# Five elementwise multiplies of a Mamba and MLP layer moved from the Vector engine to GpSimd

## The chip, the cores and the metric

The kernel runs on the 8 cores of one Trainium2 chip. Each core does the same program on its own half of one sequence, with no exchange between cores. The metric is the device time of the slowest core in microseconds (us). TensorE is called PE below, VectorE DVE, ScalarE ACT, GpSimd POOL and SyncE SP.

## The reference

One "sandwich" layer on x of shape (4, 2048, 2048), float32. LN is a layer norm without weights.

```python
# attention half: LN, then a Mamba-like block with its own layer norm, then residual
a  = LN(x)
p  = layer_norm(a, ln_w, ln_b) @ in_proj_W.T              # 2048 -> 96
u  = silu(conv1d(p, conv_w, width 3) + conv_b)
d, Bp, Cp = split(u @ x_proj_W.T, [6, 16, 16])
delta = softplus(d @ dt_proj_W.T + dt_proj_b) * 0.001
s_t = exp(delta*A) * s_(t-1) + delta*Bp*u                 # 96 x 16 states, scanned over 2048 steps
y   = sum_n(s_t * Cp) + u*D
x  = x + LN(y @ out_proj_W.T + a)
# MLP half
z  = LN(x)
w  = sum(softmax(top2(z @ router.T)))                     # one weight per token
f  = mlp(z; 8192 hidden) + mlp(z; 1024 hidden) * w        # mlp: silu(z@g.T) * (z@u.T) @ d.T
x  = x + LN(f)
```

## The kernel before

All code sits in one function, `build_program`, written against a small scheduler class `Sched`. `S.op(engine, emit, reads, writes, waits)` appends one instruction to the stream of the engine named by its first argument, and turns the reads and writes of the named resources into semaphore waits. The waits don't depend on the engine: also two instructions of one engine that depend on each other wait through a semaphore. Every engine runs its stream in the order of the program text. `S.fence()` makes every engine wait for all that came before it. Features lie on the partitions and tokens on the free axis; each core owns 1024 tokens, handled as tiles of 128x512.

The stages in order of time:

- Mixer, 0 to 443 us. The core computes the scan over 2048 tokens plus a halo, in five chunks `c` of 512. For each chunk: statistics and the input projection, then, one chunk behind (`pc = c - 1`), the convolution, the gate and the projections to `dus_bf` and `du_bf`. `du_bf` is masked by a multiply with `m96k` at L685 (`ts_`). Then a loop over 12 groups `j` of 8 channels by 16 states: PE expands delta (L707) and `du` (L714) to 128 rows; ACT makes the exponential `dA` (L711); DVE makes `dBu` from PSUM (L718), runs the scan (L722) and saves the last state (L726). For the two chunks with `pc >= 2`, whose outputs the core keeps, DVE multiplies the states by C (L730, `tj7`, written in place of `dA`) and PE sums over the states with a float32 matmul (L733). In PE's stream L733 of group j stands ahead of L707 and L714 of group j+1.
- O stage, 444 to 755 us, in two passes `hc` of 512 tokens. First part, loop `mc` of 16: output projection on PE (L815, L817); DVE scales the residual from the loaded `x_half` by a broadcast row (L823, `t_s`, into one of two buffers) and adds it to PSUM (L826); ACT casts and squares; PE sums the statistics (L762, L767). Second part, loop `k` of 16: DVE multiplies `mr_sb` by the broadcast reciprocal deviation (L841, `tx1`), POOL adds the broadcast mean term (L845, `tx2`), DVE adds the residual (L849, `tx3`). All three name one resource `r_mr` for the whole of `mr_sb`, so `tx1` of tile k+1 waits for `tx3` of tile k. The result is stored to HBM.
- Normalization stage, 755 to 836 us, in two passes of 16 tiles: an ACT-queue DMA loads a tile into one of two buffers `x2t` (L911), DVE multiplies (L914, `tz1`) and adds into the bf16 `z4_sb` (L917, `tz2`). The load into a buffer waits for `tz2` of the tile that used it last.
- Router and small MLP (836 to 1100 us), the gate and up projections of the large MLP (1100 to 1998 us), its down projection (to 2570 us), and an end stage that normalizes and writes out (to 2766 us).

POOL's stream also issues DMAs: the chunk loads (L522, called from L595) in the mixer, and the weight loads (L1003, L1005 and later).

Of the kernel before, what the change touches and what calls it, by code (L numbers as in the profile page):

```python
# [24 lines left out]
ENG_SEM = {"tensor": "s_pe", "scalar": "s_act", "vector": "s_dve",  # L25
           "gpsimd": "s_pool", "sync": "s_sy"}
# [14 lines left out]
class Sched:  # L41
    def __init__(self):
        self.ops = []
        self.cnt = {}
        self.pending = {}
        self.dma_idx = {q: 0 for q in DMA_SEMS}

    def _mk(self, eng, emit, waits, inc_sem, inc_by):
        if eng in self.pending:
            waits = list(waits) + self.pending.pop(eng)  # L50
        self.cnt[inc_sem] = self.cnt.get(inc_sem, 0) + inc_by
        tok = (inc_sem, self.cnt[inc_sem], eng)
        best = {}
        for wt in waits:
            if wt is None:
                continue
            s, v, peng = wt
            if best.get(s, -1) < v:
                best[s] = v
        wl = sorted(best.items())  # L60

        def run(e, emit=emit, wl=wl, inc=(inc_sem, inc_by)):
            for s, v in wl:
                e.wait_ge(_SEMS[s], v)
            inst = emit(e)
            inst.then_inc(_SEMS[inc[0]], inc[1])
        self.ops.append((eng, run))
        return tok

# [130 lines left out]
def build_program(debug_taps=()):  # L200
    global _SEMS
    nc = bass.Bass("TRN2", target_bir_lowering=False)
# [76 lines left out]
    du_bf = at("s_dub", (96, 512), BF16, WB0 + 4096)  # L279
    m96k = [at(f"s_m96k{i}", (96, 512), F32, WB0 + 5120 + 2048 * i) for i in range(2)]  # L280
# [107 lines left out]
    S = Sched()  # L388
# [72 lines left out]
    def tap(name, ap_src, waits, reads=(), q="sync"):  # L461
        if name in taps:
            out_toks.append(S.dma(q,
                                  lambda e, a=ap_src, d=taps[name]: e.dma_start(out=d, in_=a),
                                  reads=reads, waits=waits))

    const_toks = []
    for dst, src in [(ident, ident_h), (ones1x128, ones1x128_h),
                     (ones1x128bf, ones1x128bf_h), (ones128bf, ones128bf_h),
# [36 lines left out]
    def mm_wpsum(e):  # L506
        for k in range(KC):
# [4 lines left out]
    t_wpsum = S.op("scalar", lambda e: e.activation(wpsum_bf[:], pb[6][0:1, 0:96], AF.Copy),  # L512
                   reads=[r_pb[6]], waits=[tk])

    x3 = xT.rearrange("(k p) t -> p k t", p=128)
    t_xbf = [None] * NCHUNK

# [12 lines left out]

    for c in range(NCHUNK):
        cc = c % 2
        def mm_sx(e, cc=cc):
            for k in range(KC):
                i = e.matmul(pb[0][0:1, :], ones128bf[:], xcb[cc][:, 512 * k:512 * (k + 1)],
                             start=(k == 0), stop=(k == KC - 1))
            return i
        t_sx = S.op("tensor", mm_sx, reads=[r_xcb[cc]], writes=[r_pb[0]],
                    waits=[t_xbf[c]] + CW)
        for k in range(KC):  # L540
            kk = k % 2
# [75 lines left out]
        if c == 2:  # L617
# [8 lines left out]
        tap(f"xp{c}", xp_all[0:96, 1 + 512 * c:1 + 512 * (c + 1)], [t3_],  # L626
            reads=[r_xp[c]])

        pc = c - 1
        if pc < 0:  # L630
            continue
        pcc = pc % 2
# [49 lines left out]
        tr_ = S.op("vector", lambda e, pcc=pcc: e.scalar_tensor_tensor(  # L682
                       du_bf[:], dus_bf[:], 0.001, u_ch[pcc][:, :], ALU.mult, ALU.mult),
                   reads=[r_dus, r_u[pcc]], writes=[r_dub], waits=[tq])
        ts_ = S.op("vector", lambda e, pcc=pcc: e.tensor_mul(du_bf[:], du_bf[:], m96k[pcc][:]),  # L685
                   reads=[r_m96[pcc]], writes=[r_dub], waits=[tr_])

        tt = S.op("tensor", lambda e: e.matmul(pb[6][:, :], selBbf[:], dbc_bf[:],
# [11 lines left out]
                       reads=[r_pb[6]], writes=[r_C[pcc]], waits=[tv])  # L700

        y_last = None
        for j in range(NJ):
            jb = j % 2
            bs = 3 if jb == 0 else 6
            bs2 = 4 if jb == 0 else 7
            tj1 = S.op("tensor", lambda e, j=j, bs=bs: e.matmul(  # L707
                           pb[bs][:, :], selDbf[:, 128 * j:128 * (j + 1)], dus_bf[:],
                           start=True, stop=True),
                       reads=[r_dus], writes=[r_pb[bs]], waits=[tq])  # L710
            tj2 = S.op("scalar", lambda e, j=j, jb=jb, bs=bs: e.activation(  # L711
                           dA_b[jb][:], pb[bs][:, :], AF.Exp, scale=A2[:, j:j + 1]),
                       reads=[r_pb[bs]], writes=[r_dA[jb]], waits=[tj1, t_A2])
            tj3 = S.op("tensor", lambda e, j=j, bs2=bs2: e.matmul(  # L714
                           pb[bs2][:, :], selDbf[:, 128 * j:128 * (j + 1)], du_bf[:],
                           start=True, stop=True),
                       reads=[r_dub], writes=[r_pb[bs2]], waits=[ts_])
            tj4 = S.op("vector", lambda e, jb=jb, pcc=pcc, bs2=bs2: e.tensor_mul(  # L718
                           dBu_b[jb][:], pb[bs2][:, :], Bp_bc[pcc][:]),
                       reads=[r_pb[bs2], r_Bp[pcc]], writes=[r_dBu[jb]], waits=[tj3, tu_])  # L720
            init = 0.0 if pc == 0 else state_cols[:, j:j + 1]
            tj5 = S.op("vector", lambda e, jb=jb, init=init: e.tensor_tensor_scan(  # L722
                           xs_b[jb][:], dA_b[jb][:], dBu_b[jb][:], init, ALU.mult, ALU.add),
                       reads=[r_dA[jb], r_dBu[jb]] + ([r_state[j]] if pc > 0 else []),
                       writes=[r_xs[jb]], waits=[tj2, tj4])
            tj6 = S.op("vector", lambda e, j=j, jb=jb: e.tensor_copy(  # L726
                           state_cols[:, j:j + 1], xs_b[jb][:, 511:512]),
                       reads=[r_xs[jb]], writes=[r_state[j]], waits=[tj5])
            if pc >= 2:
                tj7 = S.op("vector", lambda e, jb=jb, pcc=pcc: e.tensor_mul(  # L730
                               prod_b[jb][:], xs_b[jb][:], C_bc[pcc][:]),
                           reads=[r_xs[jb], r_C[pcc]], writes=[r_dA[jb]], waits=[tw_, tj6])
                tj8 = S.op("tensor", lambda e, j=j, jb=jb: e.matmul(  # L733
                               pb[2][0:96, :], selR_sb[:, 96 * j:96 * (j + 1)], prod_b[jb][:],
                               start=(j == 0), stop=(j == NJ - 1)),
                           reads=[r_dA[jb]], writes=[r_pb[2]] if j == 0 else [],
                           waits=[tj7] + CW)
                if j > 0:
                    r_pb[2].w = tj8
                y_last = tj8  # L740
# [9 lines left out]
                 reads=[r_yf], writes=[r_ybf], waits=[ty1])  # L750
    tap("yf", y_f[0:96, :], [r_ybf.w], reads=[r_yf])

    S.fence()

    def stats_tile(src_f32, first, last, wtok, par=0):
# [49 lines left out]
    for hc in range(2):  # L805
# [5 lines left out]
        for mc in range(KC):  # L811
            bank = 2 if mc % 2 == 0 else 5

            def mm_op1(e, mc=mc, off=off, bank=bank):
                e.matmul(pb[bank][:, :], outTbf[:, 128 * mc:128 * (mc + 1)],  # L815
                         y_bf[:, off:off + 512], start=True, stop=False)
                return e.matmul(pb[bank][:, :], ones1x128bf[:], nm1r1bf[:, off:off + 512],  # L817
                                start=False, stop=True)
            t_op = S.op("tensor", mm_op1, reads=[r_ybf, r_nm1r1], writes=[r_pb[bank]],
                        waits=CW)  # L820
            bcb_i = bc_b if mc % 2 == 0 else bc_b2
            r_bcb_i = r_bcb if mc % 2 == 0 else r_bcb2
            t_s = S.op("vector", lambda e, mc=mc, bcb_i=bcb_i: e.tensor_mul(  # L823
                           bcb_i[:, :], x_half[:, 512 * mc:512 * (mc + 1)], bc_a[:, :]),
                       reads=[r_xhalf, r_bca], writes=[r_bcb_i], waits=[t_xh, t_r1b])
            t_mr = S.op("vector", lambda e, mc=mc, bank=bank, bcb_i=bcb_i: e.tensor_add(  # L826
                            mr_sb[:, 512 * mc:512 * (mc + 1)], pb[bank][:, :], bcb_i[:, :]),
                        reads=[r_pb[bank], r_bcb_i], writes=[r_mr] if mc == 0 else [],
                        waits=[t_op, t_s])
            if mc > 0:  # L830
                r_mr.w = t_mr
            stats_tile(mr_sb[:, 512 * mc:512 * (mc + 1)], mc == 0, mc == KC - 1, [t_mr],
                       par=mc % 2)
# [4 lines left out]
        t_nm3b = bcast(bc_b, r_bcb, row(R_T2), r_rows[R_T2], [t_nm3], 4)  # L838
        for k in range(KC):
            kk = k % 2  # L840
            tx1 = S.op("vector", lambda e, k=k: e.tensor_mul(  # L841
                           mr_sb[:, 512 * k:512 * (k + 1)], mr_sb[:, 512 * k:512 * (k + 1)],
                           bc_a[:, :]),
                       reads=[r_bca], writes=[r_mr], waits=[t_r3b])
# [57 lines left out]
    for hc in range(2):  # L902
# [6 lines left out]
        for k in range(KC):  # L909
# [1 line left out]
            trl = S.dma("scalar", lambda e, k=k, kk=kk, off=off: e.dma_start(  # L911
                            out=x2t[kk][:], in_=x2_st[k, :, off:off + 512]),
                        writes=[r_x2t[kk]], waits=[r_x2st[k]])
            tz1 = S.op("vector", lambda e, kk=kk: e.tensor_mul(  # L914
                           x2t[kk][:], x2t[kk][:], bc_a[:, :]),
                       reads=[r_bca], writes=[r_x2t[kk]], waits=[trl, t_r4b])
            tz2 = S.op("vector", lambda e, k=k, kk=kk, off=off: e.tensor_add(  # L917
# [6 lines left out]
    tap("x2st", x2_st[:, :, :].rearrange("a b c -> (a b) c"), list(r_x2st))  # L924
    tap("z4t", z4_sb[:, :], [r_z4.w], reads=[r_z4], q="gpsimd")

    snapO = S.snapshot()
    S.fence_from(snapO)
    t_lge = [None, None]
# [64 lines left out]
    tap("combt", comb_bc[:, :], [r_combbc.w], reads=[r_combbc])  # L994
    tap("lgtt", lgt_tm[:, :], [r_lgttm.w], reads=[r_lgttm])

    S.fence_from(snapO)
    t_wrg = [None] * NRI
    t_wru = [None] * NRI
# [77 lines left out]

    tap("frst", fr_st[:, :, :].rearrange("a b c -> (a b) c"), list(r_frst))

    S.fence()  # L1080
    t_stash_done = r_x2st[KC - 1]
    t_wg = [None] * NI
# [11 lines left out]
    for i in range(NI):  # L1094
# [33 lines left out]
        if i + 2 < NI:  # L1128
            sched_wdma(i + 2)

    S.fence()
    t_wd = [[None, None] for _ in range(KC)]
    t_fr = [None] * KC
# [16 lines left out]
    for dt in range(KC):  # L1150
# [68 lines left out]
        if dt + 2 < KC:  # L1219
            sched_fdma(dt + 2)  # L1220

    S.fence()
    ep_r5 = [eprow(0), eprow(1)]
    ep_nm5 = [eprow(2), eprow(3)]
# [97 lines left out]
                    fn(e)  # L1322

    es.close()
    return nc


# [24 lines left out]
```

## Time and profile before

| | |
|---|---|
| median of the two runs | 2918.3 us (2768.13 and 3068.48) |
| the profiled execution, its own time | 2767.94 us |
| its span, first to last instruction of the slowest core | 2766.4 us |
| spans of the 8 cores | 2748.4 to 2766.4 us |
| busy: PE / ACT / DVE / POOL | 1923.9 / 466.3 / 396.3 / 355.4 us |

Busy time is a sum over the span; it doesn't say which engine is waited for in a stage. The chain of waits does: it is followed back from the last instruction, at each step to what released it. In a timeline row the first number is the start, the second the duration, both in us from the start of the span; the bracket at the end gives how long the engine stood idle ahead of the instruction and what released it. The two runs of before lie 11% apart; the profiled execution is of the lower kind, and all cores of it show about the same granted clock (0.802 to 0.806).

### The profile page before, as it was taken

What the parts mean: (1) busy time and instruction counts of PE and PEld (TensorE: products, weight loads), DVE (VectorE), ACT (ScalarE), POOL (GpSimd) and SP (SyncE); (2) the same over time, 40 slices, a digit from 0 to 9 for tenths busy, and PEclk for the clock granted to TensorE, in tenths of its full rate; (3) what the DMA queues carried; (4) which work ended last, traced back from release to release, by engine and by line L of the source; (5) the groups of instructions that cost most, each with busy time, mean ns of one, the idle gap of its engine ahead of it and who ended that gap; (6) DMA issues with size and microseconds to landing.
All of it is one profiled execution on the core that took longest, in us unless ns stands there. A gap on an engine that the chain in (4) does not pass through costs nothing.

```text
span 2766.4 us, 27032 instructions; the slowest of 8 cores (2748.4 to 2766.4 us)
## 1 busy us (share of the span) xinstructions
PE 1923.9 (70%) x7719; PEld 780.5 (28%) x7719; DVE 396.3 (14%) x589; ACT 466.3 (17%) x802; POOL 355.4 (13%) x400
## 2 busy tenths in 40 slices
PE   4444533434404976999999999999888888888200
PEld 2111100000002432444444444444333333333100
DVE  0553342232352100000000000000000000000222
ACT  3333211232301111111111111111100000000100
POOL 1000000020200210222222222222200000000122
PEclk9555555555556998999999999999989999999655
DMA  7220001030131435444444444444344444343233
GB/s 113 42 31 0 0 0 61 8 115 1 64 111 38 77 77 129 83 76 77 77 77 76 77 77 77 77 77 76 69 84 91 92 92 91 86 93 73 99 137 136
DMA packets 67530, 203.23 MB, mean 73 GB/s; under 512 B 7420, under 2 KB 17789, under 8 KB 63302
## 3 DMA queue, kind: packets, MB, share of 16 engines
q0 software_dynamic: 38608, 124.49, 26.0%
q10 hardware_dynamic: 18432, 50.34, 5.1%
q1 hardware_dynamic: 10358, 26.68, 2.7%
q8 instruction: 78, 1.28, 0.2%
q14 instruction: 54, 0.44, 0.1%
HBM read 292.41 MB, written 33.55 MB: 118 GB/s over the span
## 4 chain that ended last, share of the span: by engine, by line
PE 65%; DVE 11%; DMA 9%; issue 6%; ACT 4%; POOL 3%; DVEq 0%; SPq 0%; ACTq 0%; POOLq 0%
PE pb L1103 16%; PE pb L1112 16%; PE pb L1156 5%; PE pb L1159 4%; PE pb L1171 4%; PE pb L1174 4%; DMA s_epf<-f_stash 3%; PE pb L1019 2%; PE pb L1028 2%; DVE s_xs L722 2%; PE pb L733 2%; DMA s_x2t<-x_stash 2%; PE pb L1061 2%; DMA s_rdbuf<-Wrd 2%; POOL s_mr L845 1%
## 5 line engine op out<-in xcount | busy, mean ns | idle before, releaser
L1103 PE MATMUL pb<-s_z,s_gbuf 128*128 128x512 bf16 x2048 | 464.4, 380 | 13.4 <-DMA s_ubuf<-Wu 13.4
L1112 PE MATMUL pb<-s_z,s_ubuf 128*128 128x512 bf16 x2048 | 462.9, 379 | 0.0
L1103 PEld LDWEIGHTS pb<-s_z,s_gbuf 128*128 128x128 bf16 x2048 | 200.7, 98 | 256.3 <-issue 15.8
L1112 PEld LDWEIGHTS pb<-s_z,s_ubuf 128*128 128x128 bf16 x2048 | 200.4, 98 | 241.7
L1188 DVE TENSOR_TENSOR s_fstg<-pb,s_frbuf 128x512 f32<-128x512 f32 x32 | 20.6, 686 | 1551.6 <-PE pb L1174 1551.6
L1124 POOL TENSOR_TENSOR s_h<-s_gs,s_us 128x512 bf16<-128x512 bf16 x128 | 147.1, 1149 | 678.6 <-ACT s_us L1121 678.6
L1156 PE MATMUL pb<-s_h,s_dbuf 128*128 128x512 bf16 x512 | 210.7, 411 | 17.2 <-issue 16.9
L1159 PE MATMUL pb<-s_h,s_dbuf 128*128 128x512 bf16 x512 | 209.6, 409 | 0.0
L1171 PE MATMUL pb<-s_h,s_dbuf 128*128 128x512 bf16 x512 | 194.0, 379 | 4.1 <-PE pb L1159 4.1
L1174 PE MATMUL pb<-s_h,s_dbuf 128*128 128x512 bf16 x512 | 194.0, 379 | 0.0
L1118 ACT ACTIVATE s_gs<-pb 128x512 bf16<-128x512 f32 x128 | 76.4, 597 | 378.4 <-PE pb L1103 360.5
L1121 ACT ACTIVATE s_us<-pb 128x512 bf16<-128x512 f32 x128 | 76.4, 597 | 367.8 <-PE pb L1112 367.8
L845 POOL TENSOR_TENSOR s_mr<-s_mr,s_bcb 128x512 f32<-128x512 f32 x32 | 40.4, 1262 | 550.1 <-ACT s_bcb L797 495.3
L1196 ACT ACTIVATE s_fbf<-s_fstg 128x512 bf16<-128x512 f32 x32 | 20.1, 629 | 532.2 <-DVE s_fstg L1188 530.5
L733 PE MATMUL pb<-s_dA,s_selR 128*96 128x512 f32 x48 | 47.8, 1100 | 81.9 <-DVE s_dA L730 81.9
L1061 PE MATMUL pb<-s_rh,s_rdbuf 128*128 128x512 bf16 x256 | 69.2, 438 | 31.4 <-DMA s_rdbuf<-Wrd 31.4
L1136 POOL DMA_DIRECT2D s_dbuf<-Wd x32 | 17.0, 531 | 521.0 <-PE pb L1159 314.9
L1156 PEld LDWEIGHTS pb<-s_h,s_dbuf 128*128 128x128 bf16 x512 | 53.5, 105 | 93.1 <-issue 42.7
L762 PE MATMUL pb<-s_castb,s_o128b 128*1 128x512 bf16 x32 | 18.7, 585 | 78.0 <-ACT s_castb L758 78.0
L1159 PEld LDWEIGHTS pb<-s_h,s_dbuf 128*128 128x128 bf16 x512 | 53.2, 104 | 68.2 <-issue 17.3
L1171 PEld LDWEIGHTS pb<-s_h,s_dbuf 128*128 128x128 bf16 x512 | 50.0, 98 | 70.1 <-issue 11.5
L1174 PEld LDWEIGHTS pb<-s_h,s_dbuf 128*128 128x128 bf16 x512 | 50.1, 98 | 58.5
(192 smaller groups left out, 1468.9 us busy)
## 6 DMA issues: line engine op xcount, KB each, us to landing
s_gbuf<-Wg POOLq DMA_DIRECT2D x64, 512.0 KB, 5.9
s_ubuf<-Wu POOLq DMA_DIRECT2D x64, 512.0 KB, 7.8
s_dbuf<-Wd POOLq DMA_DIRECT2D x32, 1024.0 KB, 8.5
s_xcb<-xT POOLq DMA_DIRECT2D x5, 2048.0 KB, 15.6
s_xhalf<-xT SPq DMA_DIRECT2D x2, 4096.0 KB, 14.0
x_stash<-s_x2t ACTq DMA_DIRECT2D x32, 256.0 KB, 2.0
s_x2t<-x_stash ACTq DMA_DIRECT2D x32, 256.0 KB, 2.8
fr_stash<-s_frstg ACTq DMA_DIRECT2D x16, 512.0 KB, 5.5
```

The lines of the kernel that those rows point to most:

```text
L733: tj8 = S.op("tensor", lambda e, j=j, jb=jb: e.matmul(pb[2][0:96, :], selR_sb[:, 96 * j:96 * (j + 1)], prod_b[jb][:], start=(j == 0), stop ...
L845: tx2 = S.op("gpsimd", lambda e, k=k: e.tensor_add(mr_sb[:, 512 * k:512 * (k + 1)], mr_sb[:, 512 * k:512 * (k + 1)], bc_b[:, :]), reads=[r ...
L1061: i = e.matmul(pb[bank][:, :], rdbuf[db][:, 128 * ikr:128 * (ikr + 1)], r_h_sb[:, 1024 * ikr + hof:1024 * ikr + hof + 512], start=(ikr == ...
L1103: i2 = e.matmul(pb[bg][:, :], gbuf[ib][:, 128 * k:128 * (k + 1)], z4_sb[:, 1024 * k + hof:1024 * k + hof + 512], start=(k == 0), stop=(k = ...
L1112: i2 = e.matmul(pb[bu][:, :], ubuf[ib][:, 128 * k:128 * (k + 1)], z4_sb[:, 1024 * k + hof:1024 * k + hof + 512], start=(k == 0), stop=(k = ...
L1118: tsl = S.op("scalar", lambda e, half=half, bg=bg: e.activation(gs_t[half][:], pb[bg][:, :], AF.Silu), reads=[r_pb[bg]], writes=[r_gs[half ...
L1121: tuc = S.op("scalar", lambda e, half=half, bu=bu: e.activation(us_t[half][:], pb[bu][:, :], AF.Copy), reads=[r_pb[bu]], writes=[r_us[half ...
L1124: S.op("gpsimd", lambda e, i=i, hof=hof, half=half: e.tensor_mul(h_all[:, 1024 * i + hof:1024 * i + hof + 512], gs_t[half][:], us_t[half][:]),
L1156: e.matmul(pb[b0][:, :], dbuf[0][:, 128 * ik:128 * (ik + 1)], h_all[:, 1024 * ik:1024 * ik + 512], start=(ik == 0), stop=False)
L1159: i2 = e.matmul(pb[b1][:, :], dbuf[0][:, 128 * ik:128 * (ik + 1)], h_all[:, 1024 * ik + 512:1024 * (ik + 1)], start=(ik == 0), stop=False)
L1171: e.matmul(pb[b0][:, :], dbuf[1][:, 128 * (ik - 32):128 * (ik - 31)], h_all[:, 1024 * ik:1024 * ik + 512], start=False, stop=(ik == NI - 1))
L1174: i2 = e.matmul(pb[b1][:, :], dbuf[1][:, 128 * (ik - 32):128 * (ik - 31)], h_all[:, 1024 * ik + 512:1024 * (ik + 1)], start=False, stop=(i ...
```

## The change

Five `S.op` calls change their engine from `"vector"` to `"gpsimd"`, with operands, resources and waits unchanged: L685 (4 instructions), L730 (24), L823 (32), L841 (32) and L914 (32), in all 124. The rest of the diff records a phase name and an instruction count while the program is built; it emits no instruction.

```diff
-        def run(e, emit=emit, wl=wl, inc=(inc_sem, inc_by)):
+        ph = self.phase
+
+        def run(e, emit=emit, wl=wl, inc=(inc_sem, inc_by), ph=ph, eng=eng):
+            n0 = e.bass.n_instructions() if hasattr(e, "bass") else None
             for s, v in wl:
                 e.wait_ge(_SEMS[s], v)
             inst = emit(e)
             inst.then_inc(_SEMS[inc[0]], inc[1])
+            n1 = e.bass.n_instructions() if n0 is not None else None
+            self.dbg_map[eng].append((n1 - n0 if n0 is not None else 1 + len(wl), ph))
...
-        ts_ = S.op("vector", lambda e, pcc=pcc: e.tensor_mul(du_bf[:], du_bf[:], m96k[pcc][:]),
+        ts_ = S.op("gpsimd", lambda e, pcc=pcc: e.tensor_mul(du_bf[:], du_bf[:], m96k[pcc][:]),
...
-                tj7 = S.op("vector", lambda e, jb=jb, pcc=pcc: e.tensor_mul(
+                tj7 = S.op("gpsimd", lambda e, jb=jb, pcc=pcc: e.tensor_mul(
                                prod_b[jb][:], xs_b[jb][:], C_bc[pcc][:]),
...
-            t_s = S.op("vector", lambda e, mc=mc, bcb_i=bcb_i: e.tensor_mul(
+            t_s = S.op("gpsimd", lambda e, mc=mc, bcb_i=bcb_i: e.tensor_mul(
                            bcb_i[:, :], x_half[:, 512 * mc:512 * (mc + 1)], bc_a[:, :]),
...
-            tx1 = S.op("vector", lambda e, k=k: e.tensor_mul(
+            tx1 = S.op("gpsimd", lambda e, k=k: e.tensor_mul(
                            mr_sb[:, 512 * k:512 * (k + 1)], mr_sb[:, 512 * k:512 * (k + 1)],
                            bc_a[:, :]),
...
-            tz1 = S.op("vector", lambda e, kk=kk: e.tensor_mul(
+            tz1 = S.op("gpsimd", lambda e, kk=kk: e.tensor_mul(
                            x2t[kk][:], x2t[kk][:], bc_a[:, :]),
```

## Rows read from the trace of the kernel before

**Rows 1.** The page: span, and the chain that ended last, by engine.
```profile
span 2766.4 us, 27032 instructions; the slowest of 8 cores (2748.4 to 2766.4 us)
...
PE 65%; DVE 11%; DMA 9%; issue 6%; ACT 4%; POOL 3%; DVEq 0%; SPq 0%; ACTq 0%; POOLq 0%
```

**Rows 2.** Windows: stretch, its length, busy time of each engine, clock, DMA.
```profile
240.00:318.00 78.00, 34.28 (x50) 8.22 (x49) 34.02 (x49) 12.38 (x19) 0.00 (x0) 0.50 0.00 0
...
544.00:596.00 52.00, 19.15 (x32) 2.41 (x31) 22.15 (x32) 18.77 (x33) 20.19 (x16) 0.50 0.20 77
...
749.00:796.00 47.00, 8.33 (x10) 2.49 (x10) 23.21 (x34) 4.12 (x7) 0.00 (x0) 0.50 0.29 93
796.00:836.00 40.00, 0.00 (x0) 0.00 (x0) 22.24 (x34) 1.19 (x2) 0.00 (x0) 0.50 0.37 105
...
1100.00:1998.00 898.00, 885.68 (x4096) 401.06 (x4096) 0.00 (x0) 152.85 (x256) 215.49 (x257) 0.99 0.42 76
```

**Rows 3.** Groups of instructions by form, DVE: count, busy us, mean ns, idle before.
```profile
L841 DVE TENSOR_TENSOR s_mr<-s_mr,s_bca 128x512 f32<-128x512 f32 x32 | 22.2, 693 | 9.8 <-DVE s_x2t L849 5.2 <-ACT s_bca L797 4.6
...
L914 DVE TENSOR_TENSOR s_x2t<-s_x2t,s_bca 128x512 f32<-128x512 f32 x32 | 22.1, 690 | 34.8 <-DMA s_x2t<-x_stash 34.5
...
L730 DVE TENSOR_TENSOR s_dA<-s_xs,s_C 128x512 f32<-128x512 f32 x24 | 16.6, 693 | 2.5
```

**Rows 4.** Groups of instructions by form, POOL, same columns.
```profile
L845 POOL TENSOR_TENSOR s_mr<-s_mr,s_bcb 128x512 f32<-128x512 f32 x32 | 40.4, 1262 | 550.1 <-ACT s_bcb L797 495.3 <-DVE s_mr L841 54.9
...
L1040 POOL TENSOR_TENSOR s_rhtmp<-s_gs,s_us 128x512 bf16<-128x512 bf16 x16 | 18.4, 1147 | 133.9 <-ACT s_us L1037 133.9
```

**Rows 5.** Chain of waits, group loop with `pc >= 2`: start, us, what.
```profile
262.71 0.17 DVE s_state L726
...
262.97 0.70 DVE s_dA L730
...
263.81 1.99 PE pb L733 x2
...
269.20 0.70 DVE s_dA L730
```

**Rows 6.** Timeline around the masking multiply L685.
```profile
246.32 0.69 DVE L685 TENSOR_TENSOR s_dub<-s_dub,s_m96k 96x512 bf16<-96x512 bf16 x1
...
247.26 0.58 PE L714 MATMUL pb<-s_dub,s_selDb 96*128 96x512 bf16 x1 [0.98 <-DVE s_dub L685]
```

**Rows 7.** Timeline, O stage, first part, one period.
```profile
465.32 0.68 DVE L823 TENSOR_TENSOR s_bcb<-s_xhalf,s_bca 128x512 f32<-128x512 f32 x1
...
469.69 0.69 DVE L826 TENSOR_TENSOR s_mr<-pb,s_bcb 128x512 f32<-128x512 f32 x1 [3.69 <-PE pb L817]
```

**Rows 8.** Chain of waits, O stage, second part, one period.
```profile
547.93 0.70 DVE s_x2t L849
...
548.80 0.70 DVE s_mr L841
...
549.64 1.27 POOL s_mr L845
...
551.00 0.70 DVE s_x2t L849
```

**Rows 9.** Timeline, normalization stage, first pass.
```profile
764.22 0.69 DVE L914 TENSOR_TENSOR s_x2t<-s_x2t,s_bca 128x512 f32<-128x512 f32 x1
...
765.01 0.69 DVE L917 TENSOR_TENSOR s_z<-s_x2t,s_bcb 128x512 bf16<-128x512 f32 x1
767.01 0.69 DVE L914 TENSOR_TENSOR s_x2t<-s_x2t,s_bca 128x512 f32<-128x512 f32 x1 [1.31 <-DMA s_x2t<-x_stash]
767.81 0.69 DVE L917 TENSOR_TENSOR s_z<-s_x2t,s_bcb 128x512 bf16<-128x512 f32 x1
768.76 0.69 DVE L914 TENSOR_TENSOR s_x2t<-s_x2t,s_bca 128x512 f32<-128x512 f32 x1 [0.26 <-DMA s_x2t<-x_stash]
...
771.37 0.69 DVE L914 TENSOR_TENSOR s_x2t<-s_x2t,s_bca 128x512 f32<-128x512 f32 x1 [1.12 <-DMA s_x2t<-x_stash]
```

**Rows 10.** Timeline, end stage, where POOL and DVE share a tile.
```profile
2602.47 2.34 POOL L1271 TENSOR_TENSOR s_epf<-s_epf,s_frbuf 128x1024 f32<-128x1024 f32 x1 [9.30 <-DVE s_epf L1268]
2604.91 1.23 DVE L1274 TENSOR_TENSOR s_epo<-s_epf,s_epx 128x1024 f32<-128x1024 f32 x1 [2.58 <-POOL s_epf L1271]
```

More of the change, by code:

```diff
@@ L46, in __init__ @@
         self.dma_idx = {q: 0 for q in DMA_SEMS}
+        self.phase = "init"
+        self.dbg_map = {e: [] for e in ENG_SEM}
     def _mk(self, eng, emit, waits, inc_sem, inc_by):
@@ L465, in tap @@
                                   reads=reads, waits=waits))
+    S.phase = "prolog"
     const_toks = []
@@ L513, in build_program @@
                    reads=[r_pb[6]], waits=[tk])
+    S.phase = "mixer"
     x3 = xT.rearrange("(k p) t -> p k t", p=128)
@@ L532, in build_program @@
         cc = c % 2
+        S.phase = "mstat"
         def mm_sx(e, cc=cc):
@@ L627, in build_program @@
             reads=[r_xp[c]])
+        S.phase = "postxp"
         pc = c - 1
@@ L702, in build_program @@
         y_last = None
+        S.phase = "jloop"
         for j in range(NJ):
@@ L751, in build_program @@
     tap("yf", y_f[0:96, :], [r_ybf.w], reads=[r_yf])
+    S.phase = "O"
     S.fence()
@@ L925, in build_program @@
     tap("z4t", z4_sb[:, :], [r_z4.w], reads=[r_z4], q="gpsimd")
+    S.phase = "router"
     snapO = S.snapshot()
@@ L995, in build_program @@
     tap("lgtt", lgt_tm[:, :], [r_lgttm.w], reads=[r_lgttm])
+    S.phase = "routed"
     S.fence_from(snapO)
@@ L1078, in build_program @@
     tap("frst", fr_st[:, :, :].rearrange("a b c -> (a b) c"), list(r_frst))
+    S.phase = "gu"
     S.fence()
@@ L1129, in build_program @@
             sched_wdma(i + 2)
+    S.phase = "down"
     S.fence()
@@ L1220, in build_program @@
             sched_fdma(dt + 2)
+    S.phase = "ep"
     S.fence()
@@ L1324, in build_program @@
     es.close()
+    nc._dbg_sched = S
     return nc
```

## The prediction

> **What bounds the kernel now.** I read the page's chain of waits first. PE carries 65% of it, DVE 11% and POOL 3% [rows 1], so most of the span can't be touched by a change of DVE and POOL. The windows by stage show where it can. From 1100 to 1998 us PE is busy 885.68 of 898 us at a granted clock of 0.99, and DVE has not one instruction there [rows 2]. All five edits lie ahead of 836 us, where the rows show a granted clock of 0.50, the 1.2 GHz level, and where no engine is full: in 240 to 318 us PE is busy 34 and DVE 34 of 78 us; in 544 to 596 us DVE 22 and POOL 20 of 52 us; in 749 to 836 us DVE 45 of 87 us [rows 2]. Stages in which nobody is full are bound by a chain that goes round the engines. So the question for each moved multiply is whether it is a link of that chain, not how busy DVE is. The chain of waits and the timelines of each stage answer it. The fences behind this part pass any delay on whole.
>
> **The price of one multiply.** On DVE a 128x512 float32 multiply takes 0.69 us (693, 693 and 690 ns) [rows 3]. POOL has no float32 multiply in the trace. The nearest rows are its float32 add of the same shape, 1.262 us, and its bf16 multiply, 1.147 us [rows 4]. I take the add, since element size and ports match: +0.57 us for each; with the bf16 row +0.46. Handing over costs little: DVE to POOL 0.14 us (548.80 + 0.70 to 549.64), POOL to DVE 0.09 us (549.64 + 1.27 to 551.00), DVE to DVE through a semaphore 0.17 us (547.93 + 0.70 to 548.80) [rows 8], and 0.09 us from L726 to L730 [rows 5]. POOL to POOL and POOL to PE don't occur; I take the same 0.1 to 0.15, with 0 and 0.25 as bounds.
>
> **L730, 24 instructions: on the path.** The round of the group loop is 269.20 - 262.97 = 6.23 us. L733 starts 0.14 us after L730 ends, and L707 and L714 of the next group stand behind L733 in PE's stream, so DVE's next L718 can't start early either, however free DVE is [rows 5]. Nothing covers the longer multiply: 0.57 for it and 0.05 for the hand-over from L726 (0.14 in place of 0.09), 0.62 x 24 = 14.9 us.
>
> **L685, 4 instructions: on the path.** L685 ends at 247.01 and L714 starts at 247.26, released by it [rows 6]; L714 starts the group loop. At 0.69 now and 1.15 to 1.26 on POOL that is about 0.55 each, 2.2 us. POOL's only other work there is the issue of chunk loads. Each of those waits for L591 of its own chunk, which stands in PE's stream ahead of the group loop that a multiply feeds; none is queued between a ready multiply and PE.
>
> **L823, 32 instructions: hidden, but for two.** In the steady round of 5.0 us (465.32 to 469.69, and the 0.6 us from an L826 to its L823) DVE does L823 and then stands idle 3.69 us until PE's L817 releases L826 [rows 7]. The two buffers let POOL do L823 right after the L826 before, so 1.26 us lies under some 4.3 us of other work. Only the first of each pass is exposed, since it waits for the load of `x_half`: 2 x 0.6 = 1.2 us. Without the cover all 32 would be seen, 18 us. The time that DVE gains is worth nothing, as DVE waits for PE there.
>
> **L841, 32 instructions: on the path.** The round is L849 0.70, gap 0.17, L841 0.70, gap 0.14, L845 1.27, gap 0.09: 3.07 us from 547.93 to 551.00 [rows 8]. It looks as if POOL could now do tile k+1 while DVE does tile k. It can't: L841 writes `r_mr`, which L849 of the tile before has read, so it waits for it. After the change the round is L849, hand-over, L841 on POOL, hand-over, L845, hand-over: the same three gaps, one link 0.57 longer. The first L841 of a pass is covered by the broadcast that L845 waits for. 2 x 15 rounds x 0.57 = 17.1 us. With the hand-over bounds it is 14 to 22.
>
> **L914, 32 instructions: on the path once for two tiles.** With two buffers a buffer's round is load, L914, L917, and the next load only then. From the end of L917 at 768.50 to the next L914 at 771.37 are 2.87 us for the load; the round of a pair is 771.37 - 767.01 = 4.36 us [rows 9]. After the change it is 2.87 + 1.26 + 0.10 + 0.69 = 4.92 and a little for the wait, +0.6. The other buffer's work fits between, as POOL has 2.5 us of work for a pair. Each pass has 7 rounds and an end that is 0.53 longer: 2 x (7 x 0.6 + 0.53) = 9.5 us. The weight loads behind L914 in POOL's stream wait for the last L917 anyway.
>
> **The sum.** 14.9 + 2.2 + 1.2 + 17.1 + 9.5 = 44.9 us on the profiled execution's own 2767.9 us (span 2766.4): 2812.8 us, or 1.6% longer. The median of the two runs shown, 2918.3 us, is a mean of 2768.13 and 3068.48; my numbers stand against the first, with which the profiled execution agrees.
>
> **Rival 1, slower by over 2%: POOL and DVE shut each other out in the normalization stage.** There alone the change lets a POOL instruction and a DVE instruction that reads two SBUF tensors want to run at once: L914 of the second tile of a pair on POOL and L917 of the first on DVE. In the end stage the two only alternate [rows 10], the O stage's second part is serial [rows 8], and so no row shows what an overlap costs. If whichever starts first holds the other off, POOL wins, because its next L914 needs no hand-over: L917 of the first tile then starts 1.26 us later. The pair's tiles would be loaded about 0.6 us apart; the second load needs 3.06 us against 2.87 (765.70 to 768.76) [rows 9], so it lands about 0.8 us behind the first, inside the 1.26 us of the first L914, and the clash comes back every round. That is the point which decides: a second load landing more than 1.26 us late would end it. Round: 4.36 + 0.57 + 1.26 = 6.2 us; 2 x (7 x 1.84 + 1.1) = 28 us in place of 9.5, total 63.4, 2831.3 us. For it speaks that the pair's data are nearly simultaneous; against it, that no row shows a mutual stop. The Trainium skill, "SBUF — State Buffer", section "Who interferes with whom", says that a DVE instruction with two SBUF inputs contends with a GpSimd instruction that reads SBUF, the one that starts first keeping the other out for its whole length; by it this rival would hold. No run here shows it yet.
>
> **Rival 2: multiplies at the bf16 row's price.** At 1.147 us each of the some 75 exposed multiplies saves 0.11, about 8 us: 2804 us.
>
> **Rival 3, no cost: the second part of the O stage overlaps.** If tile k+1 on POOL didn't wait for tile k on DVE, the round would be POOL's 2 x 1.26 = 2.52 us in place of 3.07, -16.5 where I have +17.1: 2779 us. The resource `r_mr` speaks against it. A gain elsewhere would need a stage that DVE bounds, and there is none [rows 2].
>
> **How the numbers follow.** Forecast 0.48, rival 1 0.40, rival 2 0.06, rival 3 0.03, and 0.03 for a larger loss (hand-overs at their upper bound, or POOL's multiply slower than its add). The predicted time is the forecast's, 2813 us. The range takes in rival 2 with the lower hand-overs (2800) and rival 1 with hand-overs 0.1 us longer at some 75 places (2839): 2800 to 2840. The forecast's own range is 2801 to 2822. Two per cent, about what a measurement of this kernel can tell from no change, lie at 2823 us. Slower by over 2%: nearly all of rival 1 and the larger loss, 0.42. Within 2%: 0.57. Faster by over 2%: 0.01.
>
> **What would show it.** L730 and L841 at POOL with a mean of 1.26 us; the group loop's round 6.85 us, the O stage's second part 3.6 us a tile; L826 still released by PE with a round of 5.0 us; the pair's round in the normalization stage 4.95 us, or 6.2 us with L917 lengthened or late if rival 1 holds; the time from the small MLP on unchanged. I am wrong if POOL's multiply is not near its add, or if the round of the O stage falls.

## The result and the profile after

The changed kernel is slower. The ratio of its time to that of before is 1.0239, with a 95% interval of 1.0207 to 1.0271; on before's 2768 us that is +66 us (57 to 75). The profiled execution of after took 2827.95 us against 2767.94, +60.0 us. The median over all eleven runs of after is 2841.97 us; some runs of both kernels are disturbed and well above the rest, which is why the ratio leaves them out. Forecast were 2813 us, a range of 2800 to 2840 us and "within 2%" as the likeliest class.

The page after: span, and the chain that ended last, by engine. It answers to [rows 1].
```profile
span 2826.3 us, 27208 instructions; the slowest of 8 cores (2809.3 to 2826.3 us)
...
PE 63%; DVE 9%; DMA 9%; issue 7%; POOL 6%; ACT 4%; DVEq 0%; POOLq 0%; SPq 0%; ACTq 0%
```
POOL's share of the chain has doubled and DVE's has fallen by less. Line numbers of after lie 11 to 13 higher than those of before in the stages of the change, since the diff adds lines: L685 is now L696, L718 is L730, L726 is L738, L730 is L742, L733 is L745, L817 is L830, L823 is L836, L826 is L839, L841 is L854, L845 is L858, L849 is L862, L914 is L927, L917 is L930. In a row of a view, "x2" counts instructions that it shows as one.

Groups of instructions by form (count, busy us, mean ns, idle before), DVE and then POOL. They answer to [rows 3, 4].
```profile
L930 DVE TENSOR_TENSOR s_z<-s_x2t,s_bcb 128x512 bf16<-128x512 f32 x32 | 36.2, 1170 | 70.2 <-POOL s_x2t L927 70.2
...
L862 DVE TENSOR_TENSOR s_x2t<-s_mr,s_xhalf 128x512 f32<-128x512 f32 x32 | 22.1, 692 | 100.9 <-POOL s_mr L858 100.9
```
```profile
L854 POOL TENSOR_TENSOR s_mr<-s_mr,s_bca 128x512 f32<-128x512 f32 x32 | 40.4, 1263 | 65.5 <-ACT s_bca L810 35.1 <-DVE s_x2t L862 30.4
...
L927 POOL TENSOR_TENSOR s_x2t<-s_x2t,s_bca 128x512 f32<-128x512 f32 x32 | 39.7, 1262 | 73.1 <-DMA s_x2t<-x_stash 73.1
...
L742 POOL TENSOR_TENSOR s_dA<-s_xs,s_C 128x512 f32<-128x512 f32 x24 | 30.3, 1262 | 131.6 <-DVE s_state L738 131.6
```
A float32 multiply of 128x512 on POOL takes what its add takes, 1.262 us. One row was not foreseen by the forecast: the add L930, which nobody moved, went from 0.69 to 1.17 us on average, while L862, which reads two SBUF tensors as well, stayed at 0.69.

Durations of the stages, worked out from the first and last starts of their lines in the trace and averaged over the eight cores, in us ("mixer" is from the first L680 to the second L744; "O stage" from the first L826 to the last L849; "normalization" from the first L914 to the last L917; differences are taken before rounding):

| stage | before | after | difference | forecast |
|---|---|---|---|---|
| mixer | 340.6 | 359.0 | +18.4 | +17.1 |
| O stage, both parts, both passes | 289.0 | 309.1 | +20.0 | +18.3 |
| normalization | 71.3 | 95.1 | +23.8 | +9.5 |
| all the rest | 2057.0 | 2055.1 | -1.8 | 0 |
| span, mean of 8 cores | 2757.9 | 2818.3 | +60.4 | +44.9 |

### The profile page after: what moved, and what is told of

Its sections match the earlier page's. It is cut to its first block, busy times and chain, and to the rows that moved or that the text cites. A ratio compares the mean times of both kernels' runs of the same rounds, so it can differ in the third digit from the quotient of the medians.

```text
span 2826.3 us, 27208 instructions; the slowest of 8 cores (2809.3 to 2826.3 us)
## 1 busy us (share of the span) xinstructions
PE 1918.6 (68%) x7719; PEld 778.2 (28%) x7719; DVE 328.4 (12%) x465; ACT 466.3 (16%) x802; POOL 510.7 (18%) x524
## 3 DMA queue, kind: packets, MB, share of 16 engines
q8 instruction: 78, 1.28, 0.2%
## 4 chain that ended last, share of the span: by engine, by line
PE 63%; DVE 9%; DMA 9%; issue 7%; POOL 6%; ACT 4%; DVEq 0%; POOLq 0%; SPq 0%; ACTq 0%
PE pb L1119 16%; PE pb L1128 16%; PE pb L1173 4%; PE pb L1176 4%; PE pb L1188 4%; PE pb L1191 4%; DMA s_epf<-f_stash 3%; PE pb L1034 2%; PE pb L1043 2%; DVE s_xs L734 2%; PE pb L745 2%; DMA s_x2t<-x_stash 2%; DMA s_rdbuf<-Wrd 2%; POOL s_mr L858 1%; POOL s_mr L854 1%
## 5 line engine op out<-in xcount | busy, mean ns | idle before, releaser
L745 PE MATMUL pb<-s_dA,s_selR 128*96 128x512 f32 x48 | 47.8, 1100 | 98.1 <-POOL s_dA L742 98.1
L1076 PE MATMUL pb<-s_rh,s_rdbuf 128*128 128x512 bf16 x256 | 60.7, 394 | 28.2 <-DMA s_rdbuf<-Wrd 25.8
L1173 PEld LDWEIGHTS pb<-s_h,s_dbuf 128*128 128x128 bf16 x512 | 53.5, 105 | 91.1 <-issue 40.5
L949 PE MATMUL pb<-s_z,s_routerTb 128*8 128x512 bf16 x32 | 9.8, 473 | 100.4 <-DVE s_z L930 99.3
L1176 PEld LDWEIGHTS pb<-s_h,s_dbuf 128*128 128x128 bf16 x512 | 53.2, 104 | 68.0 <-issue 16.6
L1289 POOL TENSOR_TENSOR s_epf<-s_epf,s_frbuf 128x1024 f32<-128x1024 f32 x16 | 37.4, 2338 | 189.5 <-DVE s_epf L1286 133.8
L1188 PEld LDWEIGHTS pb<-s_h,s_dbuf 128*128 128x128 bf16 x512 | 50.0, 98 | 70.1 <-issue 11.6
```

The lines of the kernel that those rows point to most:

```text
L745: tj8 = S.op("tensor", lambda e, j=j, jb=jb: e.matmul(pb[2][0:96, :], selR_sb[:, 96 * j:96 * (j + 1)], prod_b[jb][:], start=(j == 0), stop ...
L1076: i = e.matmul(pb[bank][:, :], rdbuf[db][:, 128 * ikr:128 * (ikr + 1)], r_h_sb[:, 1024 * ikr + hof:1024 * ikr + hof + 512], start=(ikr == ...
L1173: e.matmul(pb[b0][:, :], dbuf[0][:, 128 * ik:128 * (ik + 1)], h_all[:, 1024 * ik:1024 * ik + 512], start=(ik == 0), stop=False)
L1176: i2 = e.matmul(pb[b1][:, :], dbuf[0][:, 128 * ik:128 * (ik + 1)], h_all[:, 1024 * ik + 512:1024 * (ik + 1)], start=(ik == 0), stop=False)
L1188: e.matmul(pb[b0][:, :], dbuf[1][:, 128 * (ik - 32):128 * (ik - 31)], h_all[:, 1024 * ik:1024 * ik + 512], start=False, stop=(ik == NI - 1))
```

## The experiments

Each is an edit of the kernel before or after. Runs e1, e3 to e7 and e9 to e11 are read by stages in one profiled execution each (e6 has one more time, 3117.2 us). Stage times are means over the eight cores; in before the cores lie within 0.3 us of each other in the mixer, 2.7 in the O stage and 5.9 in the normalization (69.7 to 75.6 us). E, F, S, M, W and H are the names of the theories in the expectations.

**e1: the fifth move alone.** Before, with
```diff
-            tz1 = S.op("vector", lambda e, kk=kk: e.tensor_mul(
+            tz1 = S.op("gpsimd", lambda e, kk=kk: e.tensor_mul(
```


> The kernel before with one of the five moves alone: the normalization stage's first multiply, L914, on GpSimd. Theory E (GpSimd's L914 of one tile and VectorE's L917 of the other, which reads two SBUF tensors, shut each other out, GpSimd first): the stage, from the first L914 to the end of the last L917, grows by 22 to 26 us on every core, as between before and after, a pair's round goes from 4.4-4.9 to 6.1 us and the first L917 of a pair reads 1.5 to 1.7 us instead of 0.69. Theory F (the forecast: both run side by side): +9.5 us, round 4.95 us, L917 0.69 us. Theory M (the loss comes only in company with the other moves, for instance through the order of the waits or later loads): less than +12 us here.

Measured: 2793.6 us; normalization 98.4 us (+27.1), every other stage as before. Form group of e1, DVE:
```profile
L917 DVE TENSOR_TENSOR s_z<-s_x2t,s_bcb 128x512 bf16<-128x512 f32 x32 | 36.2, 1171 | 75.2 <-POOL s_x2t L914 75.2
```
The loss and the stretched add come with this edit alone, so M falls; F's +9.5 us is missed by a factor of almost three. E's 22 to 26 us are passed by 1 us, and the loss is 3 us more than the stage's +23.8 in after; why is open.

**e2: after without the fifth move.** After, with L927 back on `"vector"`.

> The kernel after with L914 back on VectorE, the four other moves kept. Theory E: the normalization stage falls back to 71 us (-24 us), the whole stays 38 to 42 us above before, ratio to before 1.014 to 1.016: same within 2%. Theory F: only 9.5 us come back, ratio 1.020. The other stages stay as in after: the group loop 6.90 us a round, the O stage's first part 5.1, its second 3.67 us.

Measured: 2818.2 us in the profiled execution and 2807.0 us in the one other run that a ratio would count; the other two took 3021.0 and 3115.5 us. By stages the normalization takes 70.9 us, and the span, mean of the cores, 2798.1 us, +40.2 on before's 2757.9. So the four other moves cost 40 us, and the fifth the rest; the parts add up. Two times are too few to tell E's ratio of 1.014 to 1.016 from F's 1.020, so the stages decide here.

**e3 and e4: take VectorE's second SBUF input away.** e3 is after, e4 before, both with
```diff
-                           bc_b[:, :]),
-                       reads=[r_x2t[kk], r_bcb], writes=[r_z4] ...
+                           pb[4][:, :]),
+                       reads=[r_x2t[kk], r_pb[4]], writes=[r_z4] ...
```


> The kernel after, but L917 reads the broadcast mean term straight from its PSUM bank instead of the SBUF copy, so that VectorE has one SBUF input there; the work is the same. Theory E in the form 'two SBUF inputs on VectorE against a reading GpSimd': no mutual stop any more, L917 reads 0.69 us again, the pair's round falls from 6.1 to about 5.0 us and the stage from 95 to about 81 us (-14). Theory S (VectorE is slowed or held beside any GpSimd instruction, whatever it reads): the stage stays at 95 us and L917 at 1.1 to 1.2 us mean.

> Control for the run before it: the kernel before (L914 on VectorE) with the same edit, L917's mean term read from PSUM. Both theories: no change, the stage 71 us within 2, L917 0.69 us, since nothing runs on GpSimd there. If the stage moved here, the PSUM read itself would be the cause of what that run shows.

Measured: normalization 84.7 us in e3 and 74.7 in e4, the control 3.4 us above before's 71.3 rather than within 2; the add takes 0.69 us in both. Some two thirds of the control's 3.4 us lie between the two passes: from the last L917 of the first to the first L914 of the second are 5.6 us, 3.3 in before. The edit makes the second pass's broadcast, which writes that PSUM bank, wait for the first pass's last add. Timeline of after and then of e3, one pair of tiles and the start of the next:
```profile
821.05 2.48 POOL L927 TENSOR_TENSOR s_x2t<-s_x2t,s_bca 128x512 f32<-128x512 f32 x2 [3.55 <-DMA s_x2t<-x_stash]
822.42 2.26 DVE L930 TENSOR_TENSOR s_z<-s_x2t,s_bcb 128x512 bf16<-128x512 f32 x2 [3.77 <-POOL s_x2t L927]
827.27 2.48 POOL L927 TENSOR_TENSOR s_x2t<-s_x2t,s_bca 128x512 f32<-128x512 f32 x2 [3.74 <-DMA s_x2t<-x_stash]
```
```profile
814.36 2.48 POOL L927 TENSOR_TENSOR s_x2t<-s_x2t,s_bca 128x512 f32<-128x512 f32 x2 [2.60 <-DMA s_x2t<-x_stash]
815.72 0.69 DVE L930 TENSOR_TENSOR s_z<-s_x2t,pb 128x512 bf16<-128x512 f32 x1 [3.17 <-POOL s_x2t L927]
816.94 0.69 DVE L930 TENSOR_TENSOR s_z<-s_x2t,pb 128x512 bf16<-128x512 f32 x1 [0.53 <-POOL s_x2t L927]
819.40 2.60 POOL L927 TENSOR_TENSOR s_x2t<-s_x2t,s_bca 128x512 f32<-128x512 f32 x2 [2.57 <-DMA s_x2t<-x_stash]
```
In after POOL's two multiplies run back to back and the two adds take 2.26 us in place of 1.3: the first add starts 0.1 us after the end of the first multiply but doesn't finish before the second multiply has. In e3 the same multiplies stand beside the same adds, but the add's second operand comes from PSUM, and it takes 0.69 us although it lies wholly under a multiply. The round falls from 6.2 to 5.0 us, as E said; the stage falls by 10.4 us where E had 14, since e3 also pays what the control pays. Against its control, e3 costs 10.0 us, close to the forecast's 9.5, where after costs 23.8 against before. After has a control of its own in the O stage: on the eight cores POOL's L836 overlaps the add L839, which reads PSUM and SBUF, 16 times, and that add takes 0.69 us each time. So it is not POOL's activity as such that holds DVE (S falls), but the second SBUF input.

**e11: which engine starts first.** Before, with `tz2` (the add) on `"gpsimd"` and the multiply on `"vector"`.

> The kernel before with the normalization stage's add L917 on GpSimd and its multiply L914 on VectorE, the work of one tile unchanged (0.69 + 1.26 us). Theory E, with the engine that starts first keeping the other out: now VectorE's second multiply begins without a hand-over and GpSimd's first add has to wait for it, 0.5 us instead of 1.26; round 5.3 to 5.6 us, stage 83 to 88 us, and the GpSimd add reads 1.4 us or more where it is held. Theory F: round 4.95, stage 81 us, add 1.26 us. If GpSimd always wins whatever starts first: 95 us.

Measured: 80.6 us, below E's 83 to 88 and on F's 81. Timeline of e11, from the second pair of tiles on:
```profile
776.89 0.69 DVE L914 TENSOR_TENSOR s_x2t<-s_x2t,s_bca 128x512 f32<-128x512 f32 x1 [4.19 <-DMA s_x2t<-x_stash]
777.73 1.26 POOL L917 TENSOR_TENSOR s_z<-s_x2t,s_bcb 128x512 bf16<-128x512 f32 x1 [2.69 <-DVE s_x2t L914]
778.14 1.40 DVE L914 TENSOR_TENSOR s_x2t<-s_x2t,s_bca 128x512 f32<-128x512 f32 x1 [0.56 <-DMA s_x2t<-x_stash]
779.68 1.26 POOL L917 TENSOR_TENSOR s_z<-s_x2t,s_bcb 128x512 bf16<-128x512 f32 x1 [0.69 <-DVE s_x2t L914]
782.50 0.69 DVE L914 TENSOR_TENSOR s_x2t<-s_x2t,s_bca 128x512 f32<-128x512 f32 x1 [2.96 <-DMA s_x2t<-x_stash]
783.33 1.26 POOL L917 TENSOR_TENSOR s_z<-s_x2t,s_bcb 128x512 bf16<-128x512 f32 x1 [2.39 <-DVE s_x2t L914]
784.37 0.77 DVE L914 TENSOR_TENSOR s_x2t<-s_x2t,s_bca 128x512 f32<-128x512 f32 x1 [1.19 <-DMA s_x2t<-x_stash]
```
The stop is there: a DVE multiply that starts 0.41 us into POOL's add takes 1.40 us, one that starts 1.04 us into it 0.77; both end 0.55 us after the add. But it doesn't come back at full size each round, because the second tile's load now lands over a microsecond behind the first (DVE's two multiplies start 1.25 and 1.87 us apart). The same two instructions cost +9.3 us in this order of engines and +27.1 in e1's. My expectation had the holding engine right only for the first pair, where DVE starts first and POOL's first add takes 1.46 us.

**e6: free the O stage's second part of its shared resource.** After, with one `Res()` for each tile of `mr_sb`:
```diff
-                       reads=[r_bca], writes=[r_mr], waits=[t_r3b])
+                       reads=[r_bca], writes=[r_mrk[k]], waits=[t_r3b])
```
and the same in the two instructions behind it. These three lie 4 lines lower in e6: L858 is the multiply, L862 POOL's add and L866 DVE's add.

> The kernel after with one resource for each tile of mr_sb in the O stage's second part, so that GpSimd's L841 of tile k+1 no longer waits for VectorE's L849 of tile k; this is the third rival of the prediction made real. Its round there is 3.67 us after and 3.07 before. Theory E (GpSimd and a two-input VectorE instruction shut each other out): L849 reads up to 1.9 us and the round is 3.2 to 3.6 us, so the second part still takes longer than before (3.07). Theory F (side by side): round 2.6 to 2.8 us, GpSimd's two multiplies back to back, 14 us less than before for the 32 tiles.

Measured: a round of 2.89 us, against 3.67 after and 3.07 before, between the two theories' figures. Timeline of e6:
```profile
582.07 1.26 POOL L858 TENSOR_TENSOR s_mr<-s_mr,s_bca 128x512 f32<-128x512 f32 x1
...
582.21 1.67 DVE L866 TENSOR_TENSOR s_x2t<-s_mr,s_xhalf 128x512 f32<-128x512 f32 x1 [1.22 <-POOL s_mr L862]
...
583.47 1.53 POOL L862 TENSOR_TENSOR s_mr<-s_mr,s_bcb 128x512 f32<-128x512 f32 x1
```
The add that starts 0.14 us behind POOL's multiply takes 1.67 us, and POOL's next instruction, which starts while the held add still runs, 1.53 in place of 1.26. Both are held in turn, so E's mechanism holds, but a stop costs less than the sum of both lengths: the add ends 0.55 us after the multiply it was held by (as in e11), and the next POOL instruction 1.12 us after the add, 0.14 less than its length in each case. I had put the round too high. The dependency that the prediction named (rival 3) was real; with it gone the second part is 0.18 us a tile faster than before, not the 0.55 that POOL's own 2.52 us would give.

**e7 and e10: loads out of the way.** Both before, with L914 on POOL and four load buffers in place of two (e7), and in e10 the mean term from PSUM as well.

> The kernel before with L914 on GpSimd and four buffers for the loads of the normalization stage instead of two, so that loads no longer set the round. Theory E: the two engines take turns, 3.9 to 4.1 us for a pair of tiles, 62 to 68 us for the stage. Theory F: GpSimd's 2.5 to 2.6 us for a pair, 42 to 46 us. If the loads still bind, above 66 us with gaps that end in a DMA.

> As the four-buffer run with L914 on GpSimd, but L917 reads the mean term from PSUM, so that VectorE has one SBUF input. Theory E (the stop comes with two SBUF inputs): L917 at 0.69 us, GpSimd's multiply sets the round, 1.27 us a tile, 44 to 48 us for the stage, no better than VectorE alone with four buffers (48.4). Theory S (any instruction of VectorE): as the four-buffer run with two inputs, 58.7 us.

Measured: 58.7 us in e7 and 50.1 in e10. In both the multiply is L917 and the add L920. Timeline of e10, then of e7:
```profile
770.42 12.77 POOL L917 TENSOR_TENSOR s_x2z<-s_x2z,s_bca 128x512 f32<-128x512 f32 x10 [15.40 <-DMA s_x2z<-x_stash]
```
```profile
772.64 5.81 POOL L917 TENSOR_TENSOR s_x2z<-s_x2z,s_bca 128x512 f32<-128x512 f32 x4 [15.85 <-DMA s_x2z<-x_stash]
774.00 11.66 DVE L920 TENSOR_TENSOR s_z<-s_x2z,s_bcb 128x512 bf16<-128x512 f32 x7 [9.69 <-DMA s_x2z<-x_stash]
```
When DVE reads one SBUF input (e10), POOL needs 1.28 us for a multiply here and the add 0.69. When it reads two (e7), POOL needs 1.45 and, in this stretch of seven, DVE 1.67 for an add of 0.69; over the whole stage DVE's mean is 1.44. Both stage times miss the expected windows by 2 to 3 us (e7 below, as in e6; e10 above), but S's 58.7 for e10 is excluded. DVE alone with four buffers (e8) takes 48.4 us. e10's surplus lies between the passes, 5.7 us for 3.5, as in the control e4; one pass takes 22.5 us in e10 and 22.8 in e8. So sharing the work hardly pays even without the stop: POOL's 1.26 us for its half is nearly the 1.38 us that DVE needs for both instructions.

**e5 and e9: the order of the waits.** The rounds of after held a second, smaller surplus: 6.91 us in the group loop where 6.85 was forecast, and 5.13 us in the O stage's first part where 5.03 was to stay. `_mk`, the method of `Sched` that builds an instruction, sorts its waits by the semaphore's name. e5 and e9 are after, with
```diff
-           "gpsimd": "s_pool", "sync": "s_sy"}
+           "gpsimd": "a_pool", "sync": "s_sy"}
```
and `"e_pool"` in e9.

> The kernel after with GpSimd's semaphore renamed so that every instruction waits on it first instead of after the semaphores of ACT, VectorE and PE; nothing else changes. The group loop's round is 6.90 us where 6.85 was forecast, and the O stage's first part 5.1 us a tile in place of 5.0 although L823 lies hidden there. Theory W (an instruction waits for its semaphores one after the other; a GpSimd wait that was satisfied long ago but stands last is still carried out after the late one, 0.06 to 0.08 us): O stage first part back to 5.0 to 5.05 us a tile, group loop 6.83 to 6.85, together 4 to 5 us less ahead of the normalization stage. Theory H (the hand-over between GpSimd and another engine itself is that long, or SBUF traffic of GpSimd slows the others): no change within 1 us.

> The kernel after with GpSimd's semaphore placed behind those of the DMAs but ahead of those of the other engines in each list of waits. With it placed first of all, PE's L745 began 1.2 us after the multiply it waits for instead of 0.15, since the waits on the constants' loads then came behind the late one, while VectorE's gaps fell by 0.07 us as theory W had said. Theory W: now L745 begins 0.15 us after GpSimd's multiply, the scan 0.10 us after L730 (0.17 after), L839 0.71 us after L830 starts (0.78): group loop 6.83 us, O stage first part 5.05, 4 to 5 us less than after ahead of the normalization stage. Theory H (hand-over itself longer): as after.

Measured rounds in us (median start to start, all cores): 

| | before | after | e5 | e9 |
|---|---|---|---|---|
| group loop | 6.23 | 6.91 | 7.71 | 6.84 |
| O stage, first part | 5.03 | 5.13 | 5.06 | 5.06 |
| O stage, second part | 3.07 | 3.67 | 3.95 | 3.81 |

e5 took 2856.1 us, 27 us more in the mean span than after, where I had expected 4 to 5 less. Timeline of e5 in the group loop:
```profile
261.51 1.26 POOL L742 TENSOR_TENSOR s_dA<-s_xs,s_C 128x512 f32<-128x512 f32 x1 [6.63 <-DVE s_state L738]
263.76 1.99 PE L745 MATMUL pb<-s_dA,s_selR 128*96 128x512 f32 x2 [4.84 <-POOL s_dA L742]
```
PE starts 0.99 us after POOL has ended, 0.15 in after. L745 also lists the loads of the constants, 23 transfers on eight semaphores. With POOL's name first these eight long satisfied waits came behind the late one: 0.84 us for eight. In e9 POOL stands behind the DMA names, PE's gap is 0.15 us again and DVE's scan starts 0.10 us after the end of L730 (L718 of before) in place of 0.17. But L862, L858 and others now have waits behind the late POOL one:
```profile
596.92 1.26 POOL L858 TENSOR_TENSOR s_mr<-s_mr,s_bcb 128x512 f32<-128x512 f32 x1 [0.20 <-POOL s_mr L854]
598.42 0.69 DVE L862 TENSOR_TENSOR s_x2t<-s_mr,s_xhalf 128x512 f32<-128x512 f32 x1 [3.11 <-POOL s_mr L858]
```
0.24 us from POOL to DVE where after has 0.10. The sum of e9 is after's, 2820.1 against 2818.3 us in the mean span, so its expected 4 to 5 us did not come, though the two rounds named in it did (6.84 and 5.06). W holds in kind: what stands behind the late semaphore is paid, what stands ahead is free. No one name is right for all instructions.

**e8 and e12: the opposite of the change.** e8 is before, with `tx2` (L845) and `t_e2` (L1271) on `"vector"` and four load buffers. e12 is e8 with one line behind the first fence:
```diff
     S.fence()
+    CW = []
```
(`CW` is the list of the constants' loads, repeated in many waits; the fence has waited for them.)

> The opposite of the change: the kernel before with GpSimd's two adds of the normalizing parts (L845 and L1271) on VectorE, and four load buffers in the normalization stage. From the rows of before: O stage second part from 3.07 to about 2.4 us a tile, -20 us; normalization stage from 71 to 45-50 us (2.8 us a pair, VectorE bound), -23 us; end stage, where a round of 11.3 us holds the add of 2.34 us on the path, -1.1 us for each of 16 tiles, -17 us. Together -60 us, 2707 us, ratio 0.978. A theory by which offloading VectorE is worth something in these stages expects the first and third term to be zero or a loss.

> The opposite of the change with four load buffers (2706 us) and, after the first fence, without the repeated waits on the constants' loads, which every engine has already waited for there. In the O stage's first part PE stands 0.39 and 0.61 us ahead of L767 and L815 in each round of 5.03 us, with nothing late. Theory W (each satisfied wait costs the engine time, and PE pays some eight of them): 0.8 to 0.9 us less for each of 32 tiles, the round at 4.2 us, and 2 to 3 us elsewhere: 2677 us, ratio to before 0.967 to 0.970. If those gaps have another cause, 2706 us.

Measured: e8 2706.2 us, ratio 0.9784 (0.9770 to 0.9797), 2707 expected: -21.8 us from the first L841 to the last L849, -22.8 in the normalization and -17.6 in the end stage. So the two adds moved to DVE are worth 39 us of it and the four buffers 23. e12 2639.0 us, ratio 0.9541 (0.9526 to 0.9556), 38 us better than I expected. Chains of waits, O stage first part, e8 and then e12 (L770 and L771 are L767 of before, L818 and L819 are L815):
```profile
502.14 0.39 issue
502.53 0.60 PE pb L770
503.13 0.62 issue
503.75 0.59 PE pb L818
```
```profile
506.90 0.52 PE pb L771
507.42 0.54 PE pb L819
```
The gaps on PE with nothing late are gone: the round falls from 5.03 to 3.90 us, 1.1 in place of the 0.8 to 0.9 expected. What I had missed is the down projection, where four short PE matmuls a tile carried the same list: from its first matmul to the end stage's first multiply (L1156 and L1268 of before) e8's 576.6 us became 549.6. e12 is the fastest kernel of the study, 4.6% below before.

## Why the prediction was wrong

**What bounds the kernel, and the stages after 836 us:** right. From the start of the last L917 to the end of the span the mean core took 1918.9 us before and 1917.0 after.

**Price of one multiply:** right; 1.26 to 1.27 us for each 128x512 float32 form and 1.15 us for L685, which is bf16 and 96x512, with hand-overs of 0.14 to 0.15 (POOL to PE and to itself) and 0.10 us (POOL to DVE).

**L730 and L685:** right, +18.4 us for 17.1. One round of after, chain of waits, to be read against [rows 5]:
```profile
259.34 0.17 DVE s_state L738
...
259.64 1.27 POOL s_dA L742
...
261.05 1.99 PE pb L745 x2
...
264.00 0.70 DVE s_dBu L730
```
The hand-over from the state copy is 0.13 us, as assumed; the surplus of 0.06 us a round is the scan, which now waits for POOL's semaphore behind DVE's (in e9 the round is 6.84 us).

**L823:** the cover held, L839 is still released by PE [rows 7]. "Hidden, but for two" was short by 0.10 us a tile, of which 0.07 have the same cause:
```profile
492.54 0.60 PE L830 MATMUL pb<-s_nm1r1b,s_o1xb 1*128 1x512 bf16 x1
493.32 0.69 DVE L839 TENSOR_TENSOR s_mr<-pb,s_bcb 128x512 f32<-128x512 f32 x1 [4.38 <-PE pb L830]
```
0.78 us from start to start, 0.71 before and in e5 and e9. A hidden producer on another engine still leaves its wait on the path. The other 0.03 us a tile stay in e5 and e9 (5.06 us) and are open.

**L841:** right. The round is 3.67 us for 3.64 forecast, in the shape forecast: multiply, add, add in series [rows 8].
```profile
592.45 1.26 POOL L854 TENSOR_TENSOR s_mr<-s_mr,s_bca 128x512 f32<-128x512 f32 x1 [1.00 <-DVE s_x2t L862]
...
593.86 1.27 POOL L858 TENSOR_TENSOR s_mr<-s_mr,s_bcb 128x512 f32<-128x512 f32 x1
...
595.23 0.69 DVE L862 TENSOR_TENSOR s_x2t<-s_mr,s_xhalf 128x512 f32<-128x512 f32 x1 [2.98 <-POOL s_mr L858]
```

**L914: the step that failed.** "The other buffer's work fits between, as POOL has 2.5 us of work for a pair" counted POOL's time alone: it put the overlap of POOL's multiply with DVE's add at no cost. The pair's round is 6.2 us (821.05 to 827.27) for 4.95 forecast, and the stage cost +23.8 us for 9.5. Rival 1 gave it 6.2 us a round and +28, 2831.3 us in total; the profiled execution took 2827.95. Its mechanism, the winner (POOL) and the point that decides (a second load within 1.26 us of the first) are what the runs show: e1 gives the price alone, e3 removes it by taking away the second SBUF input, and in e11, where the loads land farther apart, it is smaller. Only the form differs: the rival let the held add start 1.26 us late, while in the trace it starts on time and takes 1.66 us. The Trainium skill, "SBUF — State Buffer", "Who interferes with whom", says just this of a DVE instruction with two SBUF inputs beside a reading GpSimd instruction, and the trace agrees: 1.17 us on average for 0.69. I gave it 0.40 since no row of before could show it: on none of the eight cores does a POOL add or multiply of before run beside a DVE instruction. That is where I chose wrongly: the absence of an overlap in the trace of before is no evidence about what an overlap costs, and the edit created the first one.

The predicted range of 2800 to 2840 us holds the measured time because it was drawn to take in rival 1, not because the sum was right. With the forecast's 9.5 us in place of the 23.8, after's span would be some 14 us shorter, and the forecast's sum right within 2 us. The four other terms cost 40 us (e2) for 35.4 forecast, which makes up little of the miss. What stays open is that the ratio stands for +66 us and the profiled executions for +60; the interval (57 to 75) holds both, and no run was made on the difference.

## What to carry to other kernels

When engines wait for each other in a ring, moving an instruction that is a link of the ring to a slower engine costs its extra length each round and gains nothing, however busy the first engine was; ask who releases whom, not who is busy. Before work goes to GpSimd, list the VectorE instructions that will run beside it and read two SBUF tensors; give them a PSUM operand, or keep the work on VectorE. Here two adds moved from GpSimd to VectorE gave 39 us, 1.4% of before, and with four load buffers 2.2%. Look also at gaps called "issue" that repeat with nothing late: in this kernel needless waits on loads long done cost 2.5%.

## What the runs showed of the hardware

- A held DVE instruction with two SBUF inputs isn't delayed by the whole of POOL's length on top of its own: started 0.14 us behind a POOL multiply of 1.26 us it took 1.67 us (e6), started 0.41 us into a POOL add 1.40 us and 1.04 us into one 0.77 us (e11). In all three the DVE instruction ends 0.55 us after POOL's: it is held to the end of the other, and then needs its own length less 0.14 us.
- Waits that are already satisfied are not free when they stand behind the one that is late: eight on PE 0.84 us (e5), two on DVE 0.14 us (e9). Ahead of the late one they cost nothing that can be seen. With no late wait at all they still held PE: 0.39 and 0.61 us in each round of the O stage's first part, gone in e12.
